# Zeros, folds, the normalizing of y and the second LayerNorm's transposes moved in a one-core decoder layer

## The reference

```
h  = x + self_attention(layernorm(x))     # 16 heads of 8, in groups of 32 tokens, causal,
                                          # q and k through an rmsnorm with weight ln_w
h2 = h + cross_attention(layernorm(h), ctx)   # ctx (4, 64, 128), 16 heads of 64, own layernorm with
                                              # gamma, beta inside; output * tanh(gate), plus bias
out = h2 + moe(layernorm(h2))             # router: sigmoid, 2 of 4 groups, 4 of 16 experts, weights
                                          # normed and scaled by 2.5; 2 shared experts; silu(g) * u
```

## Time and profile before

| | us |
|---|---|
| median of 3 runs | 228.75 (227.56 to 229.52) |
| the profiled execution | 228.28 |
| its span, first to last instruction | 226.6 |
| busy in it: PE, DVE, ACT, POOL | 191.0, 164.0, 84.7, 72.4 |

### The profile page before, as it was taken

The page is one execution under the profiler, slowest core; times in us unless marked ns, Lnnn a source line. Parts: engine busy times, 40 slices in busy tenths (PEclk is TensorE's granted clock), DMA queues, the critical chain, the costliest instruction groups (busy, mean ns, idle before and its releaser), DMA issues.

```text
span 226.6 us, 5275 instructions
## 1 busy us (share of the span) xinstructions
PE 191.0 (84%) x1899; PEld 150.7 (67%) x1899; DVE 164.0 (72%) x413; ACT 84.7 (37%) x162; POOL 72.4 (32%) x148
## 2 busy tenths in 40 slices
PE   5478877999864791899998868999999999999991
PEld 5356775665653431467776746888888888888890
DVE  5743156566699456659999968999878787878783
ACT  2043567565663122346556524122323232322220
POOL 3653220011112309937765422222242224320000
PEclk9999699999998569799999996799999999999999
DMA  4994000000000001100000000011000100000003
GB/s 118 327 258 137 1 3 3 0 6 3 3 3 3 3 0 44 49 0 0 3 1 0 3 0 23 1 36 38 23 23 23 46 23 3 0 0 0 0 1 93
DMA packets 10886, 7.37 MB, mean 33 GB/s; under 512 B 1633, under 2 KB 10098, under 8 KB 10738
## 3 DMA queue, kind: packets, MB, share of 16 engines
q1 hardware_dynamic: 10000, 6.89, 10.3%
q10 hardware_dynamic: 866, 0.21, 0.4%
HBM read 6.57 MB, written 0.52 MB: 31 GB/s over the span
## 4 chain that ended last, share of the span: by engine, by line
PE 61%; DVE 18%; ACT 8%; POOL 6%; issue 3%; DMA 1%; DVEq 0%; POOLq 0%; ACTq 0%
PE banks L1298 11%; PE banks L1144 5%; PE banks L1169 4%; PE banks L1029 3%; PE banks L1191 3%; PE banks L1011 3%; PE banks L1196 3%; PE banks L1195 3%; PE banks L1193 3%; PE banks L1194 3%; PE banks L1192 3%; PE banks L1107 3%; ACT vbd L520 3%; PE banks L1158 2%; PE banks L1114 2%
## 5 line engine op out<-in xcount | busy, mean ns | idle before, releaser
L665 ACT ACTIVATE sil<-banks 128x512 f32<-128x512 f32 x36 | 21.4, 598 | 60.4 <-PE banks L1193 56.8
L966 DVE SCALAR_TENSOR_TENSOR x<-banks,combine,x 128x128 f32<-128x128 f32 x128 | 35.9, 345 | 8.9 <-PE banks L1298 8.1
L1298 PEld LDWEIGHTS banks<-dn_w,act 128*128 128x128 f32 x256 | 33.2, 191 | 2.7
L1298 PE MATMUL banks<-dn_w,act 128*128 (+1 forms) x256 | 33.4, 275 | 0.0
L950 DVE TENSOR_TENSOR act<-sil,banks 128x512 f32<-128x512 f32 x36 | 24.7, 687 | 4.3 <-ACT sil L665 1.0
L452 POOL TENSOR_TENSOR gu_hi<-gu_w,zero_col 128x256 fp32r<-128x256 f32 x18 | 11.1, 616 | 47.7 <-PE banks L1196 47.7
L378 POOL TENSOR_SCALAR ve<-mv 128x1 f32<-128x1 f32 x16 | 3.1, 197 | 60.9 <-DVE mv L679 60.9
L1144 PE MATMUL banks<-qk_fold,xn2T 128*128 128x512 f32 x32 | 18.8, 717 | 0.7 <-ACT xn2T L570 0.5
L1191 PE MATMUL banks<-x3hi,gu_lo 128*128 128x512 f32 x36 | 17.8, 494 | 1.6 <-DVE act L950 1.2
L1169 PE MATMUL banks<-vo_fold,p2T 128*128 128x128 f32 x128 | 17.5, 280 | 1.3 <-ACT p2T L585 1.3
L1169 PEld LDWEIGHTS banks<-vo_fold,p2T 128*128 128x128 f32 x128 | 15.8, 193 | 2.5 <-ACT p2T L585 2.0
(11 more groups left out here) (158 smaller groups left out, 384.0 us busy)
## 6 DMA issues: line engine op xcount, KB each, us to landing
wkv_sb<-in_L_xattn_w_kv_dram SPq DMA_DIRECT2D x1, 1024.0 KB, 8.7
gu_w<-in_L_ffn_gate_w_dram SPq DMA_DIRECT2D x16, 64.0 KB, 1.8
gu_w<-in_L_ffn_up_w_dram SPq DMA_DIRECT2D x16, 64.0 KB, 1.9
x<-in_x_dram SPq DMA_DIRECT2D x4, 128.0 KB, 4.2
wq_sb<-in_L_xattn_w_q_dram SPq DMA_DIRECT2D x1, 512.0 KB, 6.6
wout_sb<-in_L_xattn_w_out_dram SPq DMA_DIRECT2D x1, 512.0 KB, 9.8
out_dram<-x SPq DMA_DIRECT2D x8, 64.0 KB, 1.6
wqkv_sb<-in_L_attn_w_qkv_dram ACTq DMA_DIRECT2D x1, 192.0 KB, 3.2
```

The costliest lines, as they stand in the source:

```text
L665: sc.activation(sil[:, j % 2, :], bank[j % 2], ACT.Silu).then_inc(sil_s, 1)
L966: dve.scalar_tensor_tensor(out=x[:, t, :], in0=bank[4 + (j + 2) % 4][:, m * D:(m + 1) * D], scalar=combine[:, t, bass.ds(e, 1)], in1=x[:, ...
L1298: last = pe.matmul(bank[4 + (j + 2) % 4][:, m * D:(m + 1) * D], act[:, j % 4, m * P:(m + 1) * P], dn_w[:, bass.ds(n, 1), :].rearrange("p o ...
```

## The change

**The start.** The second half of `vbd`'s zeros is written by ACT, as a copy of a broadcast zero column, and not by POOL. `vbd` gets a ninth column for each head, which POOL sets to one on the head's partitions, in place of `onesbd`. The two tiles of pair 0 are loaded by two queues (SP and ACT), `w_qkv` moves to SP behind the first, five small loads move to SP. DVE's order in the first pass changes a little.

**Folds.** `ctx` and `wq` are transposed into banks 1 to 3 after `project_qk(0)` and after `transpose_q(0)`, and their copies stand there in ACT's order; `kv` 0 and 1 go between pairs 1, 2 and 3, and `A` 0 before step 0. The other units move up by half a step to one step.

**y.** `values1` has `p1T` stationary and the nine columns of `vbd` moving, so y comes out with tokens on the partitions and each head's denominator beside it. `norm_y` takes 16 reciprocals and multiplies into `yn`; PE transposes it (`transpose_y`, the last work of PE's step), ACT copies it (`copy_yT`, the last of ACT's step), and `project_out` reads that.

**Second LayerNorm.** POOL applies it as soon as its statistics are there, into `xn2`, kept for all tiles. PE transposes pairs (`transpose_xn2`) at steps 5, 6, 8 and 10, and ACT copies pairs. `values1(7)` goes behind `scores2(0)`.

**Softmax of the cross attention.** `softmax2_max(t)` stands one step earlier in DVE's list, at step t+8, before `norm_y(7)` at step 8. `exp2(t)` stays at step t+9 of ACT's.

```diff
@@ first pass
-            pool.memset(vbd[:, NT // 2:NT, :, :, :], 0.0).then_inc(vbd_zero, 1)
...
+            sc.copy(vbd[:, NT // 2:NT, :, :, :, :].rearrange("p t g r h d -> p (t g r h d)"),
+                    zero_col[:, 0:1].to_broadcast([P, NT // 2 * NG * NR * VA])).then_inc(vbd_zero, 1)
             copy_xnT(0)
             square(0)
             copy_q(0)
+            copy_fold(("ctx", 0))
             copy_xnT(1)
             square(1)
             copy_q(1)
             copy_qT(0)
+            copy_fold(("wq", 0))
             copy_xnT(2)
@@ units
+        units_before = [("ctx", 0), ("wq", 0), ("kv", 0), ("kv", 1), ("A", 0)]
         units_at = {
+            0: ([("kv", 2), ("kv", 3)], [("A", 1)]),
+            1: ([("kv", 4), ("kv", 5)], [("A", 2)]),
+            2: ([("kv", 6), ("kv", 7)], [("A", 3)]),
+            3: ([("VW", 0)], [("VW", 1)]),
+            4: ([("VW", 2)], [("VW", 3)]),
         }
@@ DVE: norm_y
             def norm_y(t):
+                y = PV[:, 0:NR * VA].rearrange("p (h d) -> p h d", d=HD + 1)
                 dve.wait_ge(y1_s, t + 1)
+                dve.reciprocal(rs1[:, t % 2, :], y[:, :, HD]).then_inc(rs1_s, 1)
+                dve.wait_ge(rs1_s, t + 1)
                 if t >= 2:
+                    dve.wait_ge(yTp_s, t - 1)
+                dve.tensor_tensor(yn[:, t % 2, :, :], y[:, :, 0:HD],
+                                  rs1[:, t % 2, :].unsqueeze(2).to_broadcast([P, H1, HD]), ALU.mult).then_inc(yn_s, 1)
@@ ACT, in a step
+                if i >= 1:
+                    copy_yT(i - 1)
@@ POOL
                     norm_scale(1, i - 2, 1.0 + LN_EPS, LN_EPS * LN_EPS)
+                    norm_apply(1, i - 2, xn2[:, i - 2, :])
...
-                if NT - 1 <= i < 2 * NT - 1:
-
-                    norm_apply(1, i - NT + 1)
@@ PE
                 for r in range(NR):
+                    for g in range(NG):
+                        last = pe.matmul(PV[QUAD * g:QUAD * (g + 1), r * VA:(r + 1) * VA],
+                                         p1T[:, t % 2, r, LS * g:LS * (g + 1)],
+                                         vbd[:, t, g, r, :, :].rearrange("p h d -> p (h d)"), start=True, stop=True)
                 last.then_inc(y1_s, 1)
...
+                if i == 5 or i == 6:
+                    transpose_xn2(i - 5)
+                if i >= 1:
+                    transpose_y(i - 1)
@@ DVE, steps
-                if i == NT + 1:
-                    softmax2_max(0)
                 if 2 <= i < NT + 2:
                     residual1(i - 2)
                 if i < NT:
                     max1_sub(i)
                 if 2 <= i < NT + 2:
                     norm_stats(1, i - 2)
+                if NT <= i < NT + 2:
+                    softmax2_max(i - NT)
                 if 1 <= i < NT + 1:
                     norm_y(i - 1)
                 if NT + 2 <= i < 2 * NT + 2:
                     softmax2_sum(i - NT - 2)
-                if NT + 2 <= i < 2 * NT + 1:
-                    softmax2_max(i - NT - 1)
+                if NT + 2 <= i < 2 * NT:
+                    softmax2_max(i - NT)
```

More of the change, by code:

```diff
@@ L427, in constants @@
             def constants():
[L429 to L435, removed]
+                pool.wait_ge(vbd_zero, 2)
+                pool.wait_ge(rqk_s, 2)
+                for h in range(HR):
+                    pool.memset(vbd[QUAD * h:QUAD * (h + 1), :, :, :, h, HD:HD + 1], 1.0).then_inc(vbd_one, 1)
+                    pool.wait_ge(vbd_one, h + 1)
                 for g in range(NG):
@@ L519, in copy_v @@
                     hs = slice(QUAD * h, QUAD * (h + 1))
[L520 removed]
+                    last = sc.copy(vbd[hs, 2 * p:2 * p + 2, :, :, h, 0:HD].rearrange("p t g r d -> p (t g r) d"),
                                    XA[p][hs, 2 * P:4 * P].rearrange("p (c d) -> p c d", d=HD))
@@ L539, in copy_p1T, with copy_yT @@
                 sc.copy(p1T[:, t % 2, :, :].rearrange("p r q -> p (r q)"), P1T).then_inc(p1Tc_s, 1)
+            def copy_yT(t):
+                sc.wait_ge(yTp_s, t + 1)
+                if t >= 2:
+                    sc.wait_ge(o1_s, t - 1)
+                sc.copy(yT[:, t % 2, :], PV[:, YTCOL:YTCOL + P]).then_inc(yT_s, 1)
             def copy_fold(u):
@@ L1037, in transpose_k, with transpose_xn2, transpose_xn3 @@
                 last.then_inc(kTp_s, 1)
-            def transpose_xn(n, t, dst):
-                pe.wait_ge(xn_s[n], t + 1)
-                pe.transpose(dst, xn[:, n - 1, t % 2, :], ident[:, :]).then_inc(xT_s[n], 1)
+            def transpose_xn2(p):
+                pe.wait_ge(xn_s[1], 2 * (p + 1))
+                if p == 0:
+                    pe.wait_ge(f_copied, len(units))
+                else:
+                    pe.wait_ge(xn2T_s, p)
+                if p == 3:
+                    pe.wait_ge(rwT_s, 1)
+                for a in range(2):
+                    last = pe.transpose(T1[:, XN2COL + a * P:XN2COL + (a + 1) * P], xn2[:, 2 * p + a, :], ident[:, :])
+                last.then_inc(xT_s[1], 1)
+            def transpose_xn3(t):
+                pe.wait_ge(xn_s[2], t + 1)
+                if t == 0:
+                    pe.wait_ge(xn2T_s, B)
+                else:
+                    pe.wait_ge(eneg_s, t)
+                pe.transpose(T1[:, X3COL:X3COL + P], xn3[:, t % 2, :], ident[:, :]).then_inc(xT_s[2], 1)
             def scores1(t):
@@ L1203, in _ @@
             project_qk(0)
+            fold(("ctx", 0))
             transpose_xn1(1)
@@ L1216, in _ @@
             transpose_q(2)
-            fold(("ctx", 0))
+            fold(("kv", 0))
             project_v(2)
@@ L1220, in _ @@
             transpose_q(3)
-            fold(("wq", 0))
+            fold(("kv", 1))
             project_v(3)
             transpose_k(3)
-            for u in units_before:
-                fold(u)
+            fold(("A", 0))
             for i in range(NT):
```

188 lines of the change are left out of this document (92 added, 96 removed).

## The result

The changed kernel takes 232.58 us in the median (231.21 to 236.48, four executions) against 228.97 for the kernel before: a ratio of 1.025, 95% interval 1.018 to 1.033. Some executions of nearly every kernel here are longer than the others; the ratios leave them out, the medians don't. Every execution after is longer than every one before, so the direction is clear. The size is less so: the interval stands for 4 to 7.5 us, the medians are 3.6 us apart, and without the one of 236.48 the executions average 232.1 against 228.8, 3.4 us or a ratio of 1.015. The profiled execution took 231.21 us, with a span of 229.4; before it was 228.28 and 226.6.

What follows compares the result with a forecast made beforehand. Bounds taken: PE-ACT round trips, then the fold-bank loop and DVE's list, POOL before the cross attention, nearly full PE and DVE in it. -1.5 + 6.3 + 0.5 = +5.3 on 228.28: 233.6, 234.0 against the median; range 229 to 239.

Steps and rivals of the forecast that it cites:

- The start: Ahead of the first pass: zeros by ACT shorten pair 0's path; -1.3 us, between -0.8 and -1.8.
- the loop: Cross attention: the maximum's subtraction waits for exp2 of its own step, a serial loop of 6.8 us against 5.08.
- The first pass: Up to scores1(0): wq and ctx +2.5, qT order -1.0, faster PE -2.7; with the start -2.5 us, thus 33.5.
- Steps 1 to 4: First attention with folds: copy_yT behind the fold's copy costs 0.5 us more per step (5.9); lead of 2.5 used up.
- Steps 5 to 7: First attention without folds: transpose of y waits for DVE, 4.15 us against 3.78; scores1(7) at 69.95 against 68.68.
- Step 8: scores2(0) ahead of values1(7), taking 3.75 us; statistics of tile 7 -1.0 us, or -2.9 if scores2(0) runs fast.
- `residual2(0)` 0.5 us later behind `transpose_p2(0)`: Step 11: the maximum also waits for scores2(3), so residual2(0) comes 5.25 us after transpose_p2(0), not 4.75: +0.5.
- Steps 11 to 16: Cross attention: steps of 6.8 us against 5.08, 33.9 from residual2(0) to norm_p2(7) where it was 27.54: +6.3.
- That the loop doesn't close: Rival, cross attention: ACT is never behind, PE's list rules at 4.93 us a step, 226.5; 10%.
- The clock: Rival, cross attention: PE's clock falls in the loop, half output2 takes 1 us more, +3 to +5, 237 to 239; 17%.
- The early gains: Rival: PE fast in first pass and scores2(0), -4 to -5 for -1.5, loop costs 6.8: 229 to 231.3; 15%.

Runs made afterwards that it cites:

- experiment 5: Changed kernel with the second half of the vbd zeros written by POOL again, as before the change: 235.17 us, no interval.
- experiment 6: Four kernels: kernel before with the start alone 223.94 us, with 17 warm-up transposes 222.77; changed kernel with ctx, wq, kv late 235.63, with 17 235.83.
- experiment 4: Changed kernel with the transpose of y behind scores1 of the next step but one, its copy first in ACT's step: 231.35 us, ratio 1.016 to before.
- experiment 2: Changed kernel with exp2 from step 11 on put first in ACT's list, the maximum left early: 226.79 us in the median, no interval.
- experiment 7: experiment 2 plus 32 identity transposes on PE at the end of step 10, in its wait for norm_p2(0): 223.67 us, ratio 0.983 to the kernel before.
- experiment 8: Changed kernel with experiments 2, 4 and 7 together: 221.41 us, ratio 0.970 to the kernel before.
- experiment 9: experiment 8 plus 8 identity transposes at the end of each of steps 5 to 7, and 17 instead of 14 before the first pass: 218.87 us, ratio 0.962.
- experiment 1: Changed kernel with the maximum and subtraction of tiles 4 to 7 one step later in DVE's list, as before the change: 225.31 us, ratio 0.989 to before.
- experiment 3: Kernel before with only the maximum and subtraction from tile 4 on one step earlier in DVE's list: 235.87 us, ratio 1.021 to the kernel before.

## Why the prediction was right, point by point

**The result** lies in the range, 1.4 us under the forecast. That it came so near is in part luck. In the profiled execution the loss is 2.8 us, where 5.3 was forecast: the lead at `scores1(0)` is 4.3 us larger than forecast, 3.3 of that are gone by `residual2(0)`, and the loop costs 1.3 less.

**The start**: right in its mechanism. DVE's pair takes 0.57 us, which I had put at 0.59. The zeros are worth 1.26 us (experiment 5), where I had 1.28. The loads and the new order around them, for which I gave 0.5 either way, are worth the other 0.8.

**The first pass** is the term most mis-sized: -2.5 forecast, -6.8 measured. Nearly all of the difference lies ahead of the projection of pair 2, which I had 1.2 us later (-1.3 and +2.5) and which came 3.0 earlier (13.07 for 16.04). 0.8 of these 4.2 us are the loads', 1.9 the pace of the first two projections (1.10 and 1.13 for 2.04 and 2.07). I took pairs 0 and 1 at the slow pace and only later ones at the fast one; all ran fast in that execution. The other 1.5 lie in transposes at full pace and in the price of `ctx` and `wq`, 2.5 in the sum and 1.2 by the distances between the first three pairs. From there to `scores1(0)` the sum has 3.7 us, and 3.8 were gained. Over the executions profiled since, `scores1(0)` of this list lies between 29.2 and 32.3, so part of the 6.8 is that execution's luck, and the forecast's 33.5 is outside all of them. With everything fast the place of the folds gains 0.9 (experiment 6). One bound was added up wrongly: -0.5 for a slow PE, where -1.3, +2.5 and -1.0 make +0.2.

**Steps 1 to 4**: the link through `copy_yT` is there, at 5.81 instead of the 5.9 forecast, in the one round of three in which y is in the loop; the two rounds before it take 4.9 (29.01, 33.93, 38.84 for the starts of the copies). From `scores1(0)` to `scores1(5)` it is 27.8 us, where the forecast has 28.1. **Steps 5 to 7**: two steps (the text says three, the sum has two), 4.54 and 4.16 us against the 4.15 worked out. Between `scores1(0)` and `scores1(7)` the change lost 3.9 us, and the steps say 3.8. Experiment 4 shows the cause of 2.2 us of these, regained at `scores1(7)`; the rest is argued.

**Step 8**: `scores2(0)` took 3.62 us at a low clock, as taken; `norm_scale(1, 7)` came 1.0 earlier against the lead at `scores1(7)`, where I had 2.3.

**`residual2(0)` 0.5 us later behind `transpose_p2(0)`**: wrong in size, 2.2 measured. The wait for `scores2(3)` was foreseen; that PE would be slow there was not. PE now comes to its wait early and stands still for 4.24 us, and behind it the transposes and `scores2(3)` take 1.7 us more than at full pace. Where PE waited for 3.52 us or less (experiments 2, 5, 7, 8 and 9), 5.25 was measured, the number that the prediction had for full pace. That the wait brings the slow pace is read across kernels and executions; no experiment changed the wait alone.

**Steps 11 to 16**, the main step: right. Steps of 6.47 us against 6.8 forecast, four waits of DVE for `exp2`, +5.0 against +6.3. The difference per step lies in the subtraction with `split_x3` (1.34 from its start to the next `residual2`, where I added 1.58) and in POOL's share (1.57 to the transpose, not 1.68). Experiments 1, 2 and 3 open the loop at either end and close it in the kernel before.

**The rivals.** That the loop doesn't close: out. The clock: it fell ahead of the loop and not in it (1.00 granted from 97 to 123), so the rival had the place wrong, though PE's pace did cost time. The early gains: they came, at nearly the size of that rival (4.2 us at `transpose_p2(0)`), and half of them were lost behind the wait at 86 to 90. The profiled execution, at 231.21, is where that rival ends; its bounds fit its terms only at that end, since -4 to -5 with a loop of 6.8 make 230.1 to 231.1. The rule of the Trainium skill (TensorE: Matmul & The Clock Gate, "What's actually happening"), that activity releases the throttle, agrees with experiment 9, where PE goes at full pace between and behind added transposes (from 60 to 75 us 1.00 was granted in 9, 0.82 in 8 and 0.55 in 4). Its use for `wq` and `ctx` between the pairs is not shown: the pass ran at either pace with them.

## What to carry to other kernels

When one engine's step is moved ahead in a software pipeline, look at which instruction of the other engine's list it now meets: through a single buffer (`s2`) the earlier subtraction met an exponential queued behind the logits, and a step of 5.08 us became 6.47. Move the producer or the consumer with it, or leave it. An instruction that depends on the slowest engine's last work should not be put last on the engine whose next work doesn't need it. And a lead is only worth something if it doesn't end as idling of TensorE: behind waits of 4.2 to 5.9 us the next transposes took 1.9 to 2.0 us for 1.1 in all five kernels that had one there. Transposes of the identity between the steps can pay although nobody reads them (experiment 9, with `scores2(0)` in 1.88 us for 3.45). Such parts should be tried one by one: here the start of the change alone was worth 2 to 3%, and the rest of it hid that.

## What the runs showed that I had not expected

The first projection after the same warm-up and nearly the same gap (0.5 to 0.8 us) took 1.10 us in some kernels' profiles and 2.05 in others; why stays open. The clock can fall in a stretch without a long wait: in experiment 4 PE's longest single wait from 55 to 64 us is 0.8 us (at the transpose of y), and 0.55 was granted from 60 to 75 us. And useless work on PE, 24 transposes in three steps and three more ahead of the pass, was worth 2.5 us (experiment 9 against 8); for the 32 of experiment 7 a gain isn't shown.
